# Head sums between tiles 0 and 1 of the second product, and UL's third tile ahead of the next image's group norm on VectorE

## The reference, cut to what matters

```python
x: (32, 384, 32, 32) fp32; 12 heads of 32 channels; n = 1024 positions
v = groupnorm(x)                                # 32 groups, no affine
w = einsum('bnc,oc->bno', v, qkv_w)             # the first product
s = sum over a head's channels of (w / |w| over n)**2    # the head sums
Pi = softmax over heads of s * temp
dots = sum over n of Pi / (sum of Pi) * w*w
u = -(w * Pi) / (1 + dots)
y = x + einsum('bnc,oc->bno', u, out_w) + out_b # the second product
```

## Time and profile before

| | us |
|---|---|
| median of 3 runs | 873.63 (873.52 to 873.78) |
| the profiled execution, its own time | 873.38 |
| its span in the trace | 871.5 |
| PE busy in the span | 855.4 (98%) |
| DVE busy | 748.8 (86%) |
| ACT busy | 526.5 (60%) |
| POOL busy | 230.9 (26%) |
| mean granted TensorE clock | 0.999 |

### The profile page before, as it was taken

The page is one execution under the profiler, slowest core; times in us unless marked ns, Lnnn a source line. Parts: engine busy times, 40 slices in busy tenths (PEclk is TensorE's granted clock), DMA queues, the critical chain, the costliest instruction groups (busy, mean ns, idle before and its releaser), DMA issues.

```text
span 871.5 us, 14048 instructions
## 1 busy us (share of the span) xinstructions
PE 855.4 (98%) x4322; PEld 682.3 (78%) x4322; DVE 748.8 (86%) x1389; ACT 526.5 (60%) x676; POOL 230.9 (26%) x105
## 2 busy tenths in 40 slices
PE   7989999999999999999999999999999999999996
PEld 6767788777788777788777788777788777788785
DVE  7799889899888889889889889888989889889667
ACT  4667556667555667556667556667556667556531
POOL 2432123332123332123332123331123332123300
PEclk9999999999999999999999999999999999999999
DMA  7324564634664544564544664544564534564423
GB/s 279 129 90 152 224 227 154 220 133 174 223 225 160 201 151 169 223 227 171 197 142 171 224 225 174 195 139 172 224 226 175 195 134 177 223 225 155 149 78 145
DMA packets 45523, 158.53 MB, mean 182 GB/s; under 512 B 20130, under 2 KB 24226, under 8 KB 37538
## 3 DMA queue, kind: packets, MB, share of 16 engines
q1 hardware_dynamic: 37264, 155.47, 48.5%
q10 hardware_dynamic: 8210, 2.59, 1.2%
HBM read 105.56 MB, written 52.49 MB: 181 GB/s over the span
## 4 chain that ended last, share of the span: by engine, by line
PE 95%; DVE 3%; issue 1%; DMA 1%; ACT 0%; DVEq 0%; ACTq 0%
PE acc L580 89%; PE scores L672 5%; DVE WS L884 1%; DMA bias<-in_L_conv_out_b 1%; DVE WV L928 0%; PE acc L563 0%; DVE UL L957 0%; ACT UH L438 0%; DVE W1L L741 0%; DVE stats L767 0%; PE acc L557 0%; DVE dots L923 0%; DVE dots L925 0%; DVE dots L921 0%; PE small L574 0%
## 5 line engine op out<-in xcount | busy, mean ns | idle before, releaser
L378 POOL TENSOR_TENSOR XL<-XN,XH 128x1024 fp32r<-128x1024 f32 x93 | 222.5, 2409 | 574.3 <-ACT XH L476 548.0
L448 ACT ACTIVATE WS<-acc 128x1024 f32<-128x1024 f32 x96 | 98.4, 1025 | 246.2 <-PE acc L580 183.5
L580 PE MATMUL acc<-UH,W2H 128*128 128x512 f32 x576 | 178.3, 391 | 2.8 <-ACT UH L438 2.8
L580 PE MATMUL acc<-XH,W1H 128*128 128x512 f32 x576 | 178.4, 391 | 0.2 <-DVE W1L L741 0.2
L580 PE MATMUL acc<-XH,W1L 128*128 128x512 f32 x576 | 177.7, 390 | 0.0
L580 PE MATMUL acc<-UH,W2L 128*128 128x512 f32 x576 | 177.6, 390 | 0.0
L965 DVE SCALAR_TENSOR_TENSOR X<-acc,bias,X 128x1024 f32<-128x1024 f32 x95 | 119.0, 1277 | 38.6 <-PE acc L580 38.4
L580 PE MATMUL acc<-UL,W2H 128*128 128x512 f32 x576 | 149.9, 396 | 0.8 <-DVE UL L957 0.8
L580 PE MATMUL acc<-XL,W1H 128*128 128x512 f32 x576 | 146.3, 390 | 0.0
L580 PEld LDWEIGHTS acc<-UL,W2H 128*128 128x128 f32 x576 | 105.5, 188 | 34.7 <-issue 12.3
L438 ACT ACTIVATE UH<-WV 128x1024 fp32r<-128x1024 f32 x96 | 98.2, 1056 | 52.8 <-DVE WV L910 33.1
(11 more groups left out here) (88 smaller groups left out, 457.3 us busy)
## 6 DMA issues: line engine op xcount, KB each, us to landing
PIB<-pi SPq DMA_DIRECT2D x96, 528.0 KB, 5.2
X<-in_x SPq DMA_DIRECT2D x31, 1536.0 KB, 6.3
out_y<-X SPq DMA_DIRECT2D x31, 1536.0 KB, 6.3
gathered<-stats_rows ACTq DMA_DIRECT2D x28, 72.0 KB, 5.2
pi<-PIT SPq DMA_DIRECT2D x96, 16.5 KB
X<-in_x SPq DMA_DIRECT2D x3, 512.0 KB, 4.7
out_y<-X SPq DMA_DIRECT2D x2, 512.0 KB, 2.7
WV<-in_L_conv_qkv_w SPq DMA_DIRECT2D x1, 576.0 KB, 6.6
```

What stands on the lines that cost most here:

```text
L378: pool.tensor_tensor(XL[:, t, :], XN[:, t, :], XH[:, t, :].bitcast(F32), ALU.subtract).then_inc(xl_done, 1)
L448: act.activation(square_tile(i, t), acc[:, t, :], ACT.Square, accum_out=sumsq[:, t:t + 1]).then_inc(squared, 1)
L580: last = pe.matmul(out[:, h * BANK:(h + 1) * BANK], w[:, k, m * P:(m + 1) * P], r[:, k, h * BANK:(h + 1) * BANK], start=(n == 0 and k == 0 ...
```

## The change

Two edits. On PE the head sums of image i move from inside tile 0 of the second product (ahead of its term (2, 0)) to the front of tile 1: behind tile 0's last six matmuls, and behind the two waits with which `second_product(i - 1, 1)` begins. On DVE `u_lo(i - 1, 2)` moves ahead of `group_norm(i + 1)`, so that it stands right behind `head_sum_weights(i)`. Steps 0 and 1 and the last product keep their own orders.

```diff
                 first_product(i, 2)
-                second_product(i - 1, 0, {(2, 0): lambda: head_sums(i)})
-
-                second_product(i - 1, 1, {})
+                second_product(i - 1, 0, {})
+                second_product(i - 1, 1, {(0, 0): lambda: head_sums(i)})
                 second_product(i - 1, 2, {})
...
                 head_sum_weights(i)
+                u_lo(i - 1, 2)
                 group_norm(i + 1)
-                u_lo(i - 1, 2)
                 group_stats(i + 2, [0])
```

## The result

The changed kernel takes 877.20 us (median of 6 runs, 876.59 to 878.51), the kernel before 873.70 beside it (6 runs, 873.26 to 874.19): a ratio of 1.0043, 95% interval 1.0031 to 1.0054. That is slower by 3.5 us, where 2.3 were forecast. The profiled execution took 877.55 us, its span 875.7, which is 4.2 more than the span before.

The account below looks back on a forecast made before the run. PE was taken as the bound, with 94% of the chain. Stalls of 1.3 (hold), 0.5 (late steps) and 0.6 (feedback) summed to 2.4 us over 873.38, forecast as 876.0 us, with an 8-in-10 range of 873.7 to 877.5.

Parts of the forecast that it names:

- The head sums' price: On PE, between the two tiles: the head sums cost 1.65 us as in the old place, change 0.
- rival 3: On PE, going into and out of the head sums costs nothing at a tile's boundary: faster, 869.6 us; chance 0.04.
- UL in an ordinary step: UL's tile 2 on DVE starts at P + 2.09, with 0.14 us of slack before term (2, 2): no stall.
- Rival 2: UL's waits for three semaphores cost more behind L847, so every loop step stalls: 878.7 to 881.5 us; chance 0.09.
- The hold: DVE's issue behind L847 in steps 2, 6, ... 26 delays UL; PE stalls 0.19 us seven times, 1.3 us.
- each part that was asked for: Signs in the trace: UL at P + 2.4, PE gaps of about 0.2 us in steps 2, 6, ... 26, instruction packet behind.
- Rival 1: DVE's hold goes with group_norm or is hidden behind L847, so only late steps stall: 874.2 us; chance 0.25.
- rival 4: Nothing at all: PE's queue covers the waits and the PIB shift is absorbed, 873.4 to 873.9 us; chance 0.07.
- The steps where DVE is late: In steps 10 and 22 DVE, late by PIB, delays UL, which has no slack there: 0.5 us.
- a feedback: Later head sums make softmax and PIB 0.25 us later, which reaches steps 10, 22 and partly 6: 0.6 us.
- a late PIB stops DVE by a microsecond: Condition for being wrong altogether: DVE stopped a microsecond where it was 0.3, as every PE stall stays in the time.
- The end: Step 31's shift is 1.37 us, but PIB's first tile was 2 us early for the last chain: nothing.

Follow-up runs that it names:

- The padding: Changed kernel with eight one-column DVE memsets run once ahead of the loop: 875.54 us, ratio 1.0022 to the kernel before.
- seventy: Changed kernel with seventy DVE memsets ahead of the loop, at three places (30, 18, 22): 873.74 us, ratio 1.0002 to the kernel before.
- the second edit alone: Kernel before with only UL's third tile moved ahead of group_norm on DVE, head sums still inside tile 0: 874.15 us, ratio 1.0005.
- its repetition: The changed kernel run once more with no edit: 876.55 us, ratio 1.0038 to the kernel before.
- 60 memsets: Changed kernel with 60 DVE memsets ahead of the loop (26, 17, 17): 874.11 us, ratio 1.0005 to the kernel before.
- the copies: Changed kernel with 62 memsets ahead of the loop and two 128-column DVE copies between head_sum_weights and UL in it: 877.85 us, ratio 1.0046.
- 8, 30, 46 and 70 memsets: Changed kernel with that many DVE memsets ahead of the loop: 875.54, 874.39, 873.76 and 873.74 us.
- the first edit alone: Kernel before with only the head sums moved between the tiles on PE, UL still behind group_norm: 903.77 us, ratio 1.0334.

## Why the prediction was right, and where its sizes were off

**The head sums' price.** Right. In their new place the block starts at P + 4.18 and takes 1.43, and the step keeps its length: 1.65 in all with its ends, and rival 3 (faster) is out.

**UL in an ordinary step.** Right: P + 2.09 to 2.10, no stall in the 19 steps without lateness, and the slack was measured at 0.147 us. Rival 2, stalls in every step, is out; UL's three waits cost nothing beyond L801's in the earlier trace rows.

**The hold.** Right in kind and place, a little short in size: 0.22 us in each of the seven, 1.5 in place of 1.3. Its profile shows each part that was asked for, the packet too. The padding and the kernel with UL one function further up show that it is a place in the program. Rival 1 had the hold go away with `group_norm` and is out, and rival 4 with it. The Trainium skill ("Runtime: NRT & Kernel Launch", section "Instruction fetch mechanics") says that the crossing is mostly hidden: by it these seven stalls would be none, and they are seven.

**The steps where DVE is late.** This is the term that was mis-sized. I had 0.5 for steps 10 and 22 as they stood in one profile of before, and 0.6 for a feedback, 1.1 together; it measured 2.25 in the first profile of after and about 0.7 in the second. By medians of two kernels that ran together and have no hold, 875.54 with eight memsets less 873.74 with seventy, it is up to 1.8 us. The lateness was read as a property of steps 10 and 22. It is one of the execution: other steps are late in each profile, but mostly the first of a body.

**Its cause.** Only a part of it was right. The chain of the prediction was: later head sums, softmax 0.25 later, PIB 0.25 later, DVE late. All but the last link came as said: L855 starts 0.24 later, at P + 5.74 (5.75 expected), PIB is issued 0.26 later, at P + 10.70, and in the second and third steps of a body it lands 0.2 to 0.4 later. But by itself this makes no first step of a body late: without packets the issue is as late, and with 60 and 70 memsets no loop step is. With the second edit alone the issue in the fourth step is 0.15 later, and the wait for PIB is 13.1 us, about that of the changed kernel's first profile, 12.7. What the prediction had left out is the 0.8 us by which the spreading takes longer in the fourth step of a body when the loop lies in three blocks; the kernel before has it too, and its slack covers it. The 0.26 comes on top of that; what each is worth in late steps isn't separated. The prediction had seen the packet behind the hold; it had not asked what the others of a body go with. That a late PIB stops DVE by a microsecond was named as what would upset the forecast; it did so in a few steps, and 1.15 of the 1.75 us by which the first profile exceeds the forecast for an execution are its.

**The number.** 877.2 lies within the forecast's range and 1.2 above the 876.0. By the rows the sum would have been 1.5 + 2.25 for this execution, and the rest is a term of 0.7 at the end against 0.4 ahead of the loop, neither of which was forecast; that the second takes back half of the first is luck.

**The end.** "Nothing" missed 0.7 us in both profiles of the changed kernel; the last section shows it.

## What to carry to other kernels

Before work is moved up to a slot where it is just in time, measure the slack of that slot and set it against the lateness of several executions, not against a mean step: here 0.14 us of slack met holds of 0.3 and lateness up to 0.7, and all but the slack came through, as the engine they delay is the bound. A pause of "issue" that shows at one place of a loop body with a packet of instructions behind it belongs to that place in the program; a few instructions ahead of the loop move it, and enough of them to bring the body into two blocks remove it. A loop whose slack hides it gains nothing from that: the kernel before has the same 28 packets, and no kernel here was faster than it.

## What the runs showed of the hardware

**A clock that fell at the end.** In the eleven profiles whose loop steps are compared here PE does the same ahead of the last product: thirty matmuls of 128 columns in 3.51 us, 2.28 us of waiting for UH, and the product starts 5.8 us behind the first of the thirty. In the first profile of the changed kernel its first eight matmuls then start 0.43 us apart and not 0.227. Three stretches of it, then one of its repetition, and one of the kernel before at the same place (columns: length, busy PE, PEld, DVE, ACT and POOL with their counts, granted TensorE clock, share of DMA, GB/s):

```profile
851.00:857.00 6.00, 3.84 (x33) 3.57 (x31) 5.33 (x9) 0.98 (x1) 0.00 (x0) 1.00 1.04 379
857.00:860.40 3.40, 3.27 (x8) 2.56 (x9) 3.26 (x10) 1.14 (x2) 0.00 (x0) 0.58 0.33 140
860.40:867.00 6.60, 6.60 (x29) 5.42 (x28) 5.19 (x8) 1.06 (x1) 0.00 (x0) 0.96 0.00 0
```

```profile
858.00:860.00 2.00, 2.00 (x6) 1.54 (x6) 1.86 (x7) 0.50 (x1) 0.00 (x0) 0.50 0.00 0
```

```profile
853.60:857.00 3.40, 3.13 (x13) 2.32 (x14) 3.23 (x10) 1.09 (x2) 0.00 (x0) 1.00 0.06 20
```

The granted clock went to the lower of its two levels for most of 3.4 us, eight matmuls started instead of thirteen, and then it was back. It happened in five of the eleven: both of the changed kernel, and those with 60 memsets, with the copies and with UL further up. In these the span ends 18.52 to 18.58 us behind the start of the last product; in the other six, the second edit alone and 8, 30, 46 and 70 memsets and the kernel before, 17.85 to 18.05. The twelfth profile, of the first edit alone, has the fall too (18.46). So the fall costs 0.7 us of the eight matmuls' 1.6; in the kernel before, at the full clock, matmuls of this stretch also stand up to 0.57 us apart. What decides it isn't shown: what PE did just before was the same in all of them, and whether the change made the fall likelier can't be said from these few.

**Three fetches without a pause beside them.** Of the five packets that go with each loop body in three blocks, only the one in the first step has a pause on DVE ahead of it. Three fall in the fourth step of a body, whose PIB takes 0.7 to 1.0 us longer from its issue to its landing than in a program that has no such packets. Open is how; open, too, are single late steps with no packet on the queue while their PIB moved (step 3 with 46 memsets, step 18 with the two copies), and why the border lies three or more instructions ahead of the pause.
